# A graph network and a mixture of experts on one core: routing and the picking of the first tile block by block inside the attention projection

## The chip, the cores and the metric

The kernel runs on one core of a Trainium2 chip. The metric is the device time of one execution in microseconds (us), median of three runs.

The engines are named as in the profile. PE (TensorE) multiplies matrices and PEld loads its weights. DVE (VectorE), ACT (ScalarE) and POOL (GpSimd) work on elements. SP (SyncE) only issues transfers here, and so do the queues of ACT and POOL.

## The reference, cut to what matters

```python
x = x + gnn(_layernorm(x), ...)                  # two graph convolutions over 10,000 edges, 625 nodes, D = 768
x = x + ffn(_layernorm(x)[None], ...)[0]

def ffn(x, ...):                                 # H = 12 heads of 64, E = 8 experts, K = 1, DF = 3072
    h = _ln(x, ln1_g, ln1_b)
    ...                                          # q, k, v, causal softmax, out
    x = x + out @ Wp + bp                        # the attention projection
    h2 = _ln(x, ln2_g, ln2_b).reshape(-1, d)
    gate_logits = h2 @ Wg
    w, sel = jax.lax.top_k(gate_logits, K)
    w = jax.nn.softmax(w, axis=-1)
    combine = jnp.zeros((n, E)).at[jnp.arange(n)[:, None], sel].add(w)
    hid = jax.nn.relu(jnp.einsum('nd,edf->enf', h2, W1) + b1[:, None, :])
    y = jnp.einsum('enf,efd->end', hid, W2) + b2[:, None, :]
    return x + jnp.einsum('ne,end->nd', combine, y)
```

## The kernel before

The 625 rows of x stand in five blocks (C = 5) of 125 rows (P = 125), one row to a partition. Every large product is made from high and low parts: a matrix a is cut into hi(a), rounded, and lo(a) = a - hi(a), and a product is three matmuls (hi hi, hi lo, lo hi). ACT makes the high parts (helper `hi`, L599), DVE the low ones (helper `lo`, L892 and L894).

There is no scheduler. Each engine has its own program, in the order in which it is written, and the engines wait for each other on counting semaphores (`s_...`). So an instruction that waits holds up all that stands behind it on its engine.

The stages are: one-hot counts of the edges and the two graph layers, the projections of q, k and v, attention, the attention projection with `Wp`, then the experts. The places that matter here:

- **Attention projection** (PE, `rows_product`, L1323): for each block 36 matmuls (72 with both parts of the rows, in two halves of 384 columns). DVE adds the residual (L1146, tile x2), takes the row statistics (L927 to L929), the root comes from ACT (L606), and the normalized block n2 is written in L931. PE turns n2 (`turn_n2`, L1589), ACT scales it with the second norm's weights (`h2_turned`, L798, tile h2T), and PE multiplies it with Wg (`gate_products`, L1596).
- **Routing**, for all five blocks at once after the last block: DVE copies the gate logits, finds maximum and index (L1158 to L1167) and makes a mark of the chosen expert (L1170). PE counts with it how many rows ahead chose the same expert (L1619, ranks, and L1622, totals). DVE computes from it each row's own place, 128 places (CAP) for each expert (L1194 to L1203), and the marks of the first tile (L1206, tile oh0).
- **First tile**: PE picks the rows of expert 0 by multiplying n2 with these marks (L1639, thirty matmuls), ACT scales them (L819, hgf) and makes the high part, DVE the low part (tiles hgh, hgl). All other tiles come through memory: POOL sends every row of n2 to its place in hs_d (L548, an indirect DMA for each block), and reads tile after tile back (L554).
- **Weights**: SP brings chunks of 128x2304 (`raw`, four buffers), 16 for each expert: eight of W1 and eight of W2. Chunk n + 4 is asked for when the low part of chunk n is made. ACT makes whi (L599), DVE wlo (L894), four buffers of each.
- **Expert tile** (`tile`): eight times W1 (PE, L1675), each result copied (ACT, L850), turned (PE, L1648 to L1662) and biased (DVE, L1258, tile bia), cut into parts (hTT), and eight times W2 (PE, L1694). The result goes to ys_d (POOL, L559).
- **Filler**: `keep_busy` (L1330) issues matmuls whose result nobody reads; TURN_BUSY is 24, CHOICE_BUSY 50.
- **The end**: POOL gathers the result rows of experts 0 to 6 (L563), DVE adds them (L1279). The last expert's result stays in PSUM: it is cut into parts, PE spreads it to the rows with turned marks (`spread_y`, L1715, tile oh7T), after it has put each row's bias b2 there with turned marks of all experts (`bias_y`, L1710, tile oh8T). DVE multiplies by the row's weight and adds the base (L1289), and SP stores the block.

## Time and profile before

| what | value |
|---|---|
| time, median of 3 runs | 928.65 us (924.72 to 932.22) |
| profiled execution, its own time | 930.92 us |
| span in the profile | 929.4 us, mean granted clock 0.971 |
| PE busy | 874.0 us (94%) |
| DVE busy | 705.7 us (76%) |
| ACT busy | 556.4 us (60%) |
| POOL busy | 90.3 us (10%) |

The span is the time from the first to the last instruction in the trace. A busy share is an average over stages with different limits. The granted clock is a share of TensorE's full 2.4 GHz.

### The profile page before, as it was taken

The page shows a single profiled execution, that of the slowest core. Times are in us where ns is not written, and L with a number is a line of the kernel's source. Part 1 is how long each engine was busy: PE and PEld are TensorE (multiplying, and loading weights), DVE is VectorE, ACT ScalarE, POOL GpSimd, SP SyncE. Part 2 cuts the span into 40 slices and gives each one's busy share as a digit, 9 for nine tenths or more (in the row PEclk, how much of TensorE's full clock was granted, in tenths as well). Part 3 has the DMA queues.
Part 4 walks back from the last instruction along what each step waited for, and adds up shares of the span by engine and source line. Part 5 has one row for each costly group of instructions (what it writes and reads, how often), then busy time and mean ns, then how long its engine had stood idle before and what let it go on. Part 6 is the DMA issues. An engine that isn't in the chain of part 4 may idle for free.

```text
span 929.4 us, 14804 instructions
## 1 busy us (share of the span) xinstructions
PE 874.0 (94%) x5460; PEld 842.0 (91%) x5460; DVE 705.7 (76%) x1060; ACT 556.4 (60%) x780; POOL 90.3 (10%) x88
## 2 busy tenths in 40 slices
PE   7999898989998888899889999999999999999998
PEld 7899897989998667689889989999999999999996
DVE  7997155784333899855559889898998989898895
ACT  5503223154323788842548778787887878787870
POOL 2000006031000400012050000000000000000041
PEclk9999788999999999999799999999999999999998
DMA  7020006348114910060189999999999999999984
GB/s 228 3 101 1 1 2 119 85 101 183 55 51 112 326 71 2 1 185 1 36 254 327 331 349 354 376 335 377 363 361 377 354 378 344 379 358 368 369 288 130
...
## 3 DMA queue, kind: packets, MB, share of 16 engines
...
## 4 chain that ended last, share of the span: by engine, by line
PE 43%; DVE 29%; DMA 13%; issue 7%; ACT 7%; SPq 0%; DVEq 0%; ACTq 0%
DVE wlo L894 14%; PE ps L1323 13%; DMA raw<-in_L_ffn_W 12%; PE ps L1499 7%; PE ps L1675 5%; PE ps L1694 5%; ACT whi L599 3%; DVE pr L1094 2%; DVE hTT L892 2%; DVE pTl L894 2%; PE ps L1352 1%; PE ps L1559 1%; DVE pr L1101 1%; DVE ohs L945 1%; DMA xs<-in_x 1%
## 5 line engine op out<-in xcount | busy, mean ns | idle before, releaser
L894 DVE TENSOR_TENSOR wlo<-raw,whi 128x2304 fp32r<-128x2304 f32 x137 | 350.9, 2570 | 23.7 <-ACT whi L599 23.5
L599 ACT ACTIVATE whi<-raw 128x2304 fp32r<-128x2304 f32 x139 | 296.2, 2132 | 83.4 <-DMA raw<-in_L_ffn_W 34.3
L1694 PE MATMUL ps<-whi,hTT 128*128 128x384 f32 x768 | 201.6, 339 | 1.0 <-ACT oh7T L599 1.0
L1694 PEld LDWEIGHTS ps<-whi,hTT 128*128 128x128 f32 x768 | 139.2, 188 | 1.2 <-ACT oh7T L599 1.2
L1675 PE MATMUL ps<-whi,hgh 128*128 128x384 f32 x384 | 134.1, 349 | 2.8 <-DVE hgl L894 2.8
L1675 PE MATMUL ps<-whi,hgl 128*128 128x384 f32 x384 | 130.3, 339 | 0.0
L1675 PE MATMUL ps<-wlo,hgh 128*128 128x384 f32 x384 | 129.8, 338 | 0.0
L1694 PE MATMUL ps<-wlo,hTT 128*128 128x384 f32 x384 | 129.0, 336 | 0.0
L1675 PEld LDWEIGHTS ps<-whi,hgh 128*128 128x128 f32 x384 | 73.3, 191 | 2.9 <-DVE hgl L894 2.9
L1675 PEld LDWEIGHTS ps<-wlo,hgh 128*128 128x128 f32 x384 | 73.2, 191 | 0.0
L1675 PEld LDWEIGHTS ps<-whi,hgl 128*128 128x128 f32 x384 | 73.0, 190 | 0.0
L1694 PEld LDWEIGHTS ps<-wlo,hTT 128*128 128x128 f32 x384 | 72.3, 188 | 0.0
L1352 PE MATMUL ps<-ohd,ohs 125*125 125x314 bf16 x400 | 58.2, 304 | 7.7 <-DVE ohd L946 5.7
L1352 PEld LDWEIGHTS ps<-ohd,ohs 125*125 125x125 bf16 x400 | 53.8, 139 | 10.9 <-DVE ohd L946 9.0
L1258 DVE TENSOR_TENSOR bia<-ps,b1T 128x384 f32<-128x384 f32 x64 | 35.6, 556 | 16.2 <-PE ps L1662 16.2
L606 ACT ACTIVATE root<-var 125x2 f32<-125x2 f32 (+2 forms) x13 | 2.7, 204 | 67.0 <-DVE var L914 66.9
L894 DVE TENSOR_TENSOR ql<-ps,qh 64x125 fp32r<-64x125 f32 (+1 forms) x66 | 21.8, 331 | 26.5 <-ACT qh L599 25.4
L1536 PE MATMUL ps<-ident,pr 125*125 125x125 f32 x168 | 30.6, 300 | 12.1 <-DVE pr L1101 7.6
L1536 PEld LDWEIGHTS ps<-ident,pr 125*125 125x125 f32 x168 | 22.4, 189 | 20.5 <-DVE pr L1101 9.5
L892 DVE SCALAR_TENSOR_TENSOR hTT<-bia,hTT 128x384 fp32r<-128x384 f32 x64 | 35.5, 554 | 5.6 <-ACT hTT L599 5.6
L599 ACT ACTIVATE qh<-ps 64x125 fp32r<-64x125 f32 (+1 forms) x66 | 20.1, 305 | 31.9 <-PE ps L1499 23.0
L756 ACT ACTIVATE pr<-pr,negmax 125x126 f32<-125x126 f32 (+4 forms) x60 | 36.0, 600 | 2.2 <-DVE negmax L1094 1.5
...
## 6 DMA issues: line engine op xcount, KB each, us to landing
raw<-in_L_ffn_W SPq DMA_DIRECT2D x128, 1152.0 KB, 6.9
...
```

Of the source, the lines that this page charges most:

```text
L599: act.activation(out_, in_, func).then_inc(s, 1)
L756: act.activation(pr[:, u % PRS, 0:n], pr[:, u % PRS, 0:n], ACT.Exp, bias=negmax[:, u % 4, :], scale=-1.0, accum_out=ssum[:, u // 2 % 2, u ...
L892: dve.scalar_tensor_tensor(out_, in_, 0.0, hi_, ALU.max, ALU.subtract).then_inc(s, 1)
L894: dve.tensor_tensor(out_, in_, hi_, ALU.subtract).then_inc(s, 1)
L1094: dve.tensor_tensor_reduce(pr[:, u % PRS, 0:n], score_rows(u)[:, 0:n], cmask[:, (C - 1 - c) * P:(C - 1 - c) * P + n], -(float(D) ** -0.5), ...
L1258: dve.tensor_tensor(bia[:, k % 2, :, :], blocks(2 + k % 2, 128, JW, CAP), bcol.rearrange("p (j o) -> p j o", o=1).broadcast_to((128, JW, C ...
L1323: ins = mm(ps[0:P, bank + half, 0:HB], l, rr, start=m == 0 and i == 0, stop=m == DC - 1 and i == 2)
L1352: ins = mm(ps[0:P, m, 0:HALF], ohs[:, i % EU, m * P:(m + 1) * P], ohd[:, i % EU, :], start=i in BOUNDS, stop=i + 1 in BOUNDS)
L1499: ins = mm(ps[:, 2 * (m % 2) + half, 0:HALF], l, rr, start=c == 0 and i == 0, stop=c == DC - 1 and i == 2)
L1536: ins = nc.tensor.transpose(turned_part(u)[:, b, :], pr[:, u % PRS, b * P:(b + 1) * P], ident[0:P, 0:P])
L1675: ins = mm(ps[0:CAP, k % 2, 0:FW], l, rr, start=m == 0 and j == 0, stop=m == DC - 1 and j == 2)
L1694: ins = mm(ps[0:CAP, 4 + half, 0:HB], l, rr, start=k == 0 and j == 0 and jj == 0, stop=k == FCH - 1 and j == JW - 1 and jj == 2)
```

## The change

The routing is done by blocks. `gate_products(c)` of blocks 0 to 2 runs in the middle of the product of block c + 2, DVE chooses (`chosen`) and places (`placed`) single blocks, PE counts ranks by blocks, and the picking matmuls of the first tile (`choice`) run by blocks too, into six banks. Half of the picked tile is scaled by DVE, and its high and low parts are made in two halves. The fillers get new places and numbers. The low parts of the first two weight chunks are made by POOL. The rest of the routing (totals, spill-over, slots for the scatter) stands on DVE behind the low part of the first tile.

The turned marks oh8T and the bias matmuls go. Instead POOL gathers for each block the bias row of its chosen expert from b2 (`bias_rows`) into x2, and DVE adds it, times the row's weight, to the base during the first tile. The row weights (an exponential on ACT, a division on DVE) are made in the first tile as well.

```diff
+POOL_LOW = 2
+HALF_IN = DC // 2
+CHOICE_BANK = (6, 7, 4, 5, 0, 1)
...
-TURN_BUSY = 24
-CHOICE_BUSY = 50
+NORM_BUSY = 40
+GATE_BUSY = 8
+SPLIT_BUSY = 30
...
+            def bias_rows(c):
+                g.wait_ge(s_oh8, 2 * c + 1)
+                g.wait_ge(s_n2, c + 1)
+                g.wait_ge(s_base, c + 1)
+                g.indirect_dma_start(out=x2[:, c, :], out_offset=None, in_=b2[:, :],
+                                     in_offset=bass.IndirectOffsetOnAxis(ap=eidx[:, c:c + 1], axis=0)
+                                     ).then_inc(s_b2g[c], 16)
+            for c in range(C):
+                g.wait_ge(s_x2, c + 1)
+                gp.tensor_tensor(base[:, c, :], base[:, c, :], x2[:, c, :], ALU.add).then_inc(s_base, 1)
+                if c >= 2:
+                    bias_rows(c - 2)
+            for n in range(POOL_LOW):
+                g.wait_ge(s_mhi, n + 1)
+                gp.tensor_tensor(wlo[n][:, :], raw[n][:, :], whi[n][:, :], ALU.subtract).then_inc(s_mlo, 1)
             g.wait_ge(s_zero, 16 * (TILES + 2 + K_OVER))
             g.wait_ge(s_slot, 1)
             g.wait_ge(s_n2, C)
             for c in range(C):
                 g.indirect_dma_start(out=hs_d[:, :], out_offset=bass.IndirectOffsetOnAxis(ap=slot[:, c:c + 1], axis=0),
                                      in_=n2[:, c, :], in_offset=None).then_inc(s_scat, 16)
+            for c in range(C - 2, C):
+                bias_rows(c)
...
             for c in range(C):
-                root_of()
                 if c >= 1:
                     h2_turned(c - 1)
-            h2_turned(C - 1)
+                root_of()
             a.wait_ge(s_x2, C)
             split_hi(0, 0)
-            a.wait_ge(s_oh8, 1)
-            act.activation(rt[:, 7, 0:C], rt[:, 6, 0:C], ACT.Exp).then_inc(s_act, 1)
+            h2_turned(C - 1)
             split_hi(1, 0)
             split_hi(2, 0)
...
-            tile_part(1, range(DC))
-            tile_hi(DC)
-            split_hi(3, 0)
+            a.wait_ge(s_hgT, 1)
+            for m in range(HALF_IN):
+                act.activation(hgf[:, m, :], first_in(m), ACT.Identity, scale=lnT[:, 2 * DC + m:2 * DC + m + 1],
+                               bias=lnT[:, 3 * DC + m:3 * DC + m + 1]).then_inc(s_hga, 1)
+            a.wait_ge(s_hga, HALF_IN)
+            hi(hg[0][:, 0:HALF_IN, :], hgf[:, 0:HALF_IN, :], s_hgh)
+            a.wait_ge(s_hgb, DC - HALF_IN)
+            hi(hg[0][:, HALF_IN:, :], hgf[:, HALF_IN:, :], s_hgh)
...
                             a.wait_ge(s_scat, 16 * C)
                         hi(hTT_part(0, k - 2), bia[:, k % 2, :, :], s_hTh2, ACT.Relu)
-                    if first and k - 2 == OVER_N2:
+                    if first and k == FCH:
+                        a.wait_ge(s_oh8, 2 * C)
+                        act.activation(rt[:, 7, 0:C], rt[:, 6, 0:C], ACT.Exp).then_inc(s_act, 1)
+                    if first and k == FCH + 6:
                         a.wait_ge(s_ohT, 1)
-                        hi(oh8T[0:E, :, :], blocks(4, E, C, P), s_ohl)
-                        hi(oh7T[:, :, :], blocks(6, 128, C, P), s_ohl)
+                        hi(oh7T[:, :, :], blocks(0, 128, C, P), s_ohl)
...
-            a.wait_ge(s_b2in, 16)
-            a.wait_ge(s_used, SCH * (E - 1) + FCH + 6)
-            hi(b2h, bc[1][0:E, :], s_b2h)
...
+            def chosen(c):
+                d.wait_ge(s_gate, c + 1)
+                dve.tensor_copy(lg[:, c, :], ps[0:P, 2, c * E:(c + 1) * E]).then_inc(s_lg, 1)
+                d.wait_ge(s_lg, c + 1)
+                step(dve.max(mx8[:, c, :], lg[:, c, :]))
+                step(dve.max_index(ix8[:, c, :], mx8[:, c, :], lg[:, c, :]))
+                step(dve.tensor_copy(ef5[:, c:c + 1], ix8[:, c, 0:1]))
+                dve.tensor_copy(eidx[:, c:c + 1], ix8[:, c, 0:1])
+                for to in (ohb, ohe):
+                    dve.tensor_scalar(to[:, c, :], iota8[:, :], ef5[:, c:c + 1], None, ALU.is_equal).then_inc(s_oh8, 1)
+            def placed(c0, c1):
+                d.wait_ge(s_rank, c1)
+                d.wait_ge(s_oh8, 2 * c1)
+                dve.tensor_tensor(prod[:, c0:c1, :], rank8[:, c0:c1, :], ohe[:, c0:c1, :], ALU.mult
+                                  ).then_inc(s_rkread, c1 - c0)
+                d.wait_ge(s_rkread, c1)
+                step(dve.reduce_sum(rank[:, c0:c1], prod[:, c0:c1, :], AX))
+                step(dve.scalar_tensor_tensor(own[:, c0:c1], ef5[:, c0:c1], float(CAP), rank[:, c0:c1],
+                                              ALU.mult, ALU.add))
+                for c in range(c0, c1):
+                    dve.tensor_scalar(oh0[:, c, :], iotac[:, :], own[:, c:c + 1], None, ALU.is_equal).then_inc(s_oh0, 1)
+            normed_rows(0)
+            normed_rows(1)
+            chosen(0)
+            normed_rows(2)
+            chosen(1)
+            normed_rows(3)
+            chosen(2)
+            normed_rows(4)
+            d.wait_ge(s_iotac, 1)
+            placed(0, 3)
+            chosen(3)
+            placed(3, 4)
+            chosen(4)
+            placed(4, 5)
+            d.wait_ge(s_hgT, 1)
+            for m in range(HALF_IN, DC):
+                dve.tensor_scalar(hgf[:, m, :], first_in(m), lnT[:, 2 * DC + m:2 * DC + m + 1],
+                                  lnT[:, 3 * DC + m:3 * DC + m + 1], ALU.mult, ALU.add).then_inc(s_hgb, 1)
+            for i, part in enumerate((slice(0, HALF_IN), slice(HALF_IN, DC))):
+                d.wait_ge(s_hgh, i + 1)
+                lo(hg[1][:, part, :], hgf[:, part, :], hg[0][:, part, :], s_hgl)
+            d.wait_ge(s_rank, C + 1)
...
-            split_lo(1, 0)
-            split_lo(2, 0)
-            tile_in(1)
-            for c in range(C):
-                dve.tensor_scalar(oh0[:, c, :], iotac[:, :], float(CAP * (E - 1)), own[:, c:c + 1],
-                                  ALU.add, ALU.is_equal).then_inc(s_ohe, 1)
-            split_lo(3, 0)
+            d.wait_ge(s_mlo, POOL_LOW)
...
+                    if first and k == FCH + 2:
+                        for c in range(C):
+                            dve.tensor_scalar(oh0[:, c, :], iotac[:, :], float(CAP * (E - 1)), own[:, c:c + 1],
+                                              ALU.add, ALU.is_equal).then_inc(s_ohe, 1)
+                        d.wait_ge(s_act, 1)
+                        step(dve.reciprocal(rt[:, 7, 8:8 + C], rt[:, 7, 0:C]))
+                        step(dve.tensor_tensor(wtok[:, :], rt[:, 7, 0:C], rt[:, 7, 8:8 + C], ALU.mult))
+                    if first and FCH + 3 <= k < FCH + 3 + C:
+                        c = k - FCH - 3
+                        d.wait_ge(s_base, c + 1)
+                        d.wait_ge(s_b2g[c], 16)
+                        dve.scalar_tensor_tensor(base[:, c, :], x2[:, c, :], wtok[:, c:c + 1], base[:, c, :],
+                                                 ALU.mult, ALU.add).then_inc(s_base2, 1)
...
+                d.wait_ge(s_base2, c + 1)
                 d.wait_ge(s_yg[c], 16)
                 dve.scalar_tensor_tensor(base[:, c, :], x2[:, c, :], wtok[:, c:c + 1], base[:, c, :],
                                          ALU.mult, ALU.add).then_inc(s_yin, 1)
+            for c in range(C - 1):
+                others_y(c)
             for half in range(2):
                 d.wait_ge(s_yh, half + 1)
                 part = slice(half * HB, (half + 1) * HB)
                 lo(wlo[0][0:CAP, part], ps[0:CAP, 4 + half, 0:HB], whi[0][0:CAP, part], s_yl)
-            d.wait_ge(s_yin, C)
-            for c in range(C):
+            others_y(C - 1)
+            for c in range(C):
+                d.wait_ge(s_yin, c + 1)
...
+            def ranks(c):
+                pe.wait_ge(s_oh8, 2 * c + 1)
+                if c >= 3:
+                    pe.wait_ge(s_rkread, c)
+                for b in range(c + 1):
+                    ins = mm(ps[0:P, 3, c * E:(c + 1) * E], before[:, :] if b == c else onesb[:, :], ohb[:, b, :],
+                             start=b == 0, stop=b == c)
+                ins.then_inc(s_rank, 1)
+            def choice(c, part):
+                pe.wait_ge(s_oh0, c + 1)
+                for m in part:
+                    ins = mm(first_in(m), n2[:, c, m * 128:(m + 1) * 128], oh0[:, c, :], start=c == 0, stop=c == C - 1)
                 return ins
+            def busy(n, bank):
+                keep_busy(n, onesb[:, :], onesb[:, :], bank)
             pe.wait_ge(s_wg, 16)
             for c in range(C):
                 if c >= 2:
                     pe.wait_ge(s_x2, c - 1)
-                rows_product(q, 2 * WP, c, 4 + 2 * (c % 2), None if c else {DC - 1: (s_pvl, 2 * STEPS)}).then_inc(s_wp, 1)
-                if c >= 2:
-                    gate_products(c - 2)
+                rows_product(q, 2 * WP, c, 4 + 2 * (c % 2), None if c else {DC - 1: (s_pvl, 2 * STEPS)},
+                             (lambda b=c - 2: gate_products(b)) if c >= 2 else None).then_inc(s_wp, 1)
                 if c >= 1:
                     turn_n2(c - 1)
-            keep_busy(TURN_BUSY, onesb[:, :], onesb[:, :], 3)
-            turn_n2(C - 1)
-            gate_products(C - 2)
-            gate_products(C - 1).then_inc(s_gate, 1)
-            keep_busy(TURN_BUSY, onesb[:, :], onesb[:, :], 3)
-            pe.wait_ge(s_oh8, 1)
-            ohb = rt[:, 4, 0:C * E // 2].bitcast(BF16).rearrange("p (c e) -> p c e", e=E)
-            for c in range(C):
-                for b in range(c + 1):
-                    mm(ps[0:P, 3, c * E:(c + 1) * E], before[:, :] if b == c else onesb[:, :], ohb[:, b, :],
-                       start=b == 0, stop=b == c)
+                if c >= 2:
+                    ranks(c - 2)
+            pe.wait_ge(s_x2, 4)
+            busy(NORM_BUSY, 7)
+            gate_products(3)
+            turn_n2(4)
+            busy(GATE_BUSY, 7)
+            pe.wait_ge(s_x2, C)
+            choice(0, range(4))
+            ranks(3)
+            choice(1, range(4))
+            gate_products(4)
+            choice(2, range(4))
+            for c in range(3):
+                choice(c, range(4, DC))
+            ranks(4)
+            pe.wait_ge(s_lg, C)
             for b in range(C):
-                ins = mm(ps[0:P, 3, C * E:(C + 1) * E], onesb[:, :], ohb[:, b, :], start=b == 0, stop=b == C - 1)
+                ins = mm(ps[0:P, 2, C * E:(C + 1) * E], onesb[:, :], ohb[:, b, :], start=b == 0, stop=b == C - 1)
             ins.then_inc(s_rank, 1)
+            choice(3, range(DC))
+            choice(4, range(DC)).then_inc(s_hgT, 1)
+            pe.wait_ge(s_rkread, C)
+            busy(SPLIT_BUSY, 3)
...
-            def bias_y(c, half):
-                for i, t in enumerate((b2h, b2l)):
-                    mm(ps[0:P, LAST_BANK[c] + half, 0:HB], oh8T[0:E, c, :], t[:, half * HB:(half + 1) * HB],
-                       start=i == 0, stop=False)
             def spread_y(c, half):
                 for i, t in enumerate((whi[0], wlo[0])):
                     ins = mm(ps[0:P, LAST_BANK[c] + half, 0:HB], oh7T[:, c, :], t[0:CAP, half * HB:(half + 1) * HB],
-                             start=False, stop=i == 1)
+                             start=i == 0, stop=i == 1)
                 return ins
-            pe.wait_ge(s_b2l, 1)
-            pe.wait_ge(s_hga, DC * (E + 1))
-            for c in range(3):
-                for half in range(2):
-                    bias_y(c, half)
+            pe.wait_ge(s_ohl, 1)
+            pe.wait_ge(s_hga, DC * E + HALF_IN)
```

POOL, from the residual sums to the sending of the rows; before:

```order
L538 TENSOR_TENSOR base<-base,x 125x768 [waits x2_made] x4
L542 IOTA iotac 125x128 [waits heads_done]
L548 DMA hs_d<-n,slot 1664x768 [waits n2_made,rows_chosen,hs_zeroed]
L548 DMA hs_d<-n,slot 1664x768 x4
L554 DMA hs<-hs_d 128x768 [waits tile_turned,tokens_sent]
```

and now:

```order
L558 TENSOR_TENSOR base<-base,x 125x768 [waits x2_made]
L552 DMA x<-in_L_ffn_b,eidx 125x768 [waits base_made,n2_made,choice_made]
L563 TENSOR_TENSOR wlo<-raw,whi 128x2304 [waits expert_hi] x2
L568 DMA hs_d<-n,slot 1664x768 [waits n2_made,rows_chosen,hs_zeroed]
L568 DMA hs_d<-n,slot 1664x768 x4
L552 DMA x<-in_L_ffn_b,eidx 125x768 [waits base_made,n2_made,choice_made] x2
L576 DMA hs<-hs_d 128x768 [waits tile_turned,tokens_sent]
```

Two low parts and five gathers of bias rows have come in, two of these gathers behind the scatter.

DVE, from the choice of the experts to the marks of the first tile; before, five blocks at once, with a low part of the weights in between:

```order
L1170 TENSOR_TENSOR rt<-iota,rt 125x40
L1175 RECIPROCAL rt<-rt 125x5 [waits scalar_steps,choice_made]
L1176 TENSOR_TENSOR wtok<-rt 125x5 [waits vector_steps]
L894 TENSOR_TENSOR wlo<-raw,whi 128x2304 [waits expert_hi]
L1194 TENSOR_TENSOR rt<-ps,capk 125x32 [waits ranks_done]
L1196 TENSOR_TENSOR rt<-ps,rt 125x40
L1197 TENSOR_REDUCE rt<-rt 125x8 [waits vector_steps]
L1198 TENSOR_REDUCE rt<-rt 125x5
L1201 TENSOR_TENSOR tp<-tri,rt 125x64 [waits vector_steps]
L1203 SCALAR_TENSOR_TENSOR rt<-rt 125x5
L1206 TENSOR_SCALAR oh<-iotac,rt 125x128 [waits slots_numbered,vector_steps]
```

and now, the placing of blocks 0 to 2 and the choosing of block 3:

```order
L1202 TENSOR_TENSOR rt<-ps,rt 125x24 [waits ranks_done,choice_made,slots_numbered]
L1205 TENSOR_REDUCE rt<-rt 125x3 [waits ranks_read]
L1206 SCALAR_TENSOR_TENSOR rt<-rt 125x3 [waits vector_steps]
L1209 TENSOR_SCALAR oh<-iotac,rt 125x128 [waits vector_steps]
L1209 TENSOR_SCALAR oh<-iotac,rt 125x128 x2
L1189 COPY rt<-ps 125x8 [waits gates_done]
L1191 MAX rt<-rt 125x8 [waits gates_read]
L1192 MAX_INDEX rt<-rt 125x8 [waits vector_steps]
L1193 CAST rt<-rt 125x1 [waits vector_steps]
L1194 CAST eidx<-rt 125x1 [waits vector_steps]
L1196 TENSOR_SCALAR rt<-iota,rt 125x8 x2
```

The step L1206 (now) computes the own places from two tiles in SBUF; the marks L1209 follow it. The low part of the weights is gone from between them.

DVE in the second half of the first tile (the chunks of W2), now:

```order
L1310 TENSOR_SCALAR oh<-iotac,rt 125x128 x5
L1313 RECIPROCAL rt<-rt 125x5 [waits scalar_steps]
L1314 TENSOR_TENSOR wtok<-rt 125x5 [waits vector_steps]
L917 TENSOR_TENSOR wlo<-raw,whi 128x2304 [waits expert_hi,vector_steps]
L1319 SCALAR_TENSOR_TENSOR base<-x,wtok,base 125x768 [waits b2_in0,base_made]
```

Before, only low parts stood there; the marks of the last expert and the row weights were made ahead of or early in the tile, and the base additions with bias rows did not exist.

## Rows read from the trace of the kernel before

**Rows 1.** Busy time by stretch: head, tile 0 in two parts, a middle tile
```profile
core 0: us, PE busy (x) PEld busy (x) DVE busy (x) ACT busy (x) POOL busy (x), PEclk, DMA share, GB/s
444.60:475.20 30.60, 25.15 (x249) 24.81 (x248) 18.68 (x66) 16.07 (x26) 11.19 (x6) 0.83 0.35 106
475.20:506.60 31.40, 30.39 (x176) 29.64 (x176) 25.13 (x26) 22.22 (x24) 4.93 (x3) 0.95 0.93 306
506.60:534.10 27.50, 27.50 (x162) 27.43 (x163) 22.58 (x13) 20.66 (x18) 0.58 (x1) 1.00 0.96 329
...
649.30:703.20 53.90, 53.55 (x319) 52.89 (x318) 49.10 (x35) 43.75 (x41) 1.08 (x2) 1.00 1.03 364
```

**Rows 2.** Chain of waits, 444 to 488: start us, us, what
```profile
444.58 0.97 DVE x L1146
...
447.27 2.08 ACT h2T L798 x6
...
452.60 2.53 PE ps L1596 x12
...
459.82 4.49 PE ps L1330 x50
464.31 6.77 PE ps L1639 x60
471.10 2.21 ACT hgf L819 x6
...
475.22 8.09 PE ps L1675 x36
...
484.70 3.13 PE ps L1675 x18
```

**Rows 3.** Timeline of ACT and DVE, 447 to 466: start us, us, instruction
```profile
447.06 0.20 ACT L606 ACTIVATE root<-var 125x1 f32<-125x1 f32 x1 [5.95 <-DVE var L914]
...
448.08 0.68 DVE L931 TENSOR_SCALAR n<-x,mv,rstd 125x768 f32<-125x768 f32 x1
...
452.41 2.15 ACT L599 ACTIVATE whi<-raw 128x2304 fp32r<-128x2304 f32 x1
...
460.47 0.19 DVE L1196 TENSOR_TENSOR rt<-ps,rt 125x40 f32<-125x40 f32 x1
...
461.35 1.07 DVE L1206 TENSOR_SCALAR oh<-iotac,rt 125x128 f32<-125x128 f32 x5
...
465.09 5.01 DVE L894 TENSOR_TENSOR wlo<-raw,whi 128x2304 fp32r<-128x2304 f32 x2
```

**Rows 4.** POOL and DVE side by side (timelines; xN rows: ns min/median/max, first and last start)
```profile
L538 POOL TENSOR_TENSOR base<-base,x x5: 1812/1830/1843, 416.1 to 445.6; 125x768 f32<-125x768 f32 x5
...
179.81 2.14 POOL L510 TENSOR_TENSOR xf<-xf,bc 125x768 f32<-125x768 f32 x1 [22.85 <-DVE n L1058]
...
180.88 1.02 DVE L1036 SCALAR_TENSOR_TENSOR xs<-ps,dinv,xs 125x768 f32<-125x768 f32 x1 [0.63 <-PE ps L1323]
...
193.02 2.21 POOL L510 TENSOR_TENSOR xf<-xf,bc 125x768 f32<-125x768 f32 x1 [4.75 <-DVE n L1058]
...
193.44 2.58 DVE L894 TENSOR_TENSOR hTl<-aff,hTh 128x750 fp32r<-128x750 f32 x1
...
L894 DVE TENSOR_TENSOR hTl<-aff,hTh x5: 934/943/2584, 193.4 to 215.6; 128x750 fp32r<-128x750 f32 x5
...
L894 DVE TENSOR_TENSOR wlo<-raw,whi x2: 3367/3782/4197, 143.4 to 146.7; 128x2304 fp32r<-128x2304 f32 x2
```

**Rows 5.** Timeline of DVE in tile 0: bias steps of two chunks in a row, end
```profile
491.67 0.56 DVE L1258 TENSOR_TENSOR bia<-ps,b1T 128x384 f32<-128x384 f32 x1
...
495.13 0.56 DVE L1258 TENSOR_TENSOR bia<-ps,b1T 128x384 f32<-128x384 f32 x1
...
533.87 0.55 DVE L1246 COPY ysb<-ps 128x384 f32<-128x384 f32 x1
```

**Rows 6.** Chain of waits, the end
```profile
913.95 2.30 PE ps L1710 x12
...
924.82 1.02 DVE base L1289
```

134 lines of the change are left out of this document (53 added, 81 removed).

## The prediction

> **What bounds the kernel now.** I read first the table of stretches [rows 1], for who is busy in which stage, then the chain of waits through the routing [rows 2] and at the end [rows 6], then the timeline of the engines for the steps that are moved [rows 3, 5], and last the places where POOL and DVE compute at the same time [rows 4].
>
> In a middle expert (649.3 to 703.2) TensorE is busy 53.55 of 53.9 us and DVE only 49.10; DMA shows a share above 1 at 364 GB/s. A started expert stage is bound by TensorE, with little room in the DMA, and a shift of its start goes through to the end if the weights keep up. From 444.6 to 475.2 no expert work is done: DMA share 0.35, granted clock 0.83. That TensorE is "busy" there is mostly filler, 4.49 us of it in one row [rows 2]. The chain goes from the last block's sum (444.58) through normalization, gate products (2.53 us at the lower clock), ranks, the picking of the first tile (6.77 us), its scaling on ACT (2.21 us) and its high and low parts to the first expert matmul at 475.22. That is 30.6 us. What this change can gain is there, in tile 0 behind it, and in the end after 913.95.
>
> **The head, step by step.** (a) Routing of blocks 0 to 2 is now done inside the projection. The fifth product has one more gate product in front of it (half of 2.53 us, so 1.25) and three rank matmuls (fillers of like form take 4.49/50 = 0.09 us each), with waits some 1.9 us. So it ends near 446.5 and not 444.58. (b) On ACT the last root now stands behind the scaling of block 3 (2.1 us, [rows 2]), which costs some 0.6 us more: root at 449.6 for 447.06, and the last normalized block, which was done 1.70 us after the root's start (448.08 + 0.68, [rows 3]), is done at 451.3 for 448.76. (c) Ranks by marks and own slots took 460.47 to 462.42 for five blocks [rows 3]; for the first three 1.4 us, so their first-tile marks could be ready at 452.7. (d) What is left per block is small: choosing (copy, maximum, index, marks) 1.2 us and placing 0.9 us on DVE, and on TensorE 0.23 us for each of the thirty picking matmuls (6.77/30). Most of them run while DVE chooses; behind the last mark only the last block's six stand, and ahead of those block 3's six. With nothing else in the way I come to a tile picked at 462.7. (e) Behind it half of the scaling goes to DVE (three of six on each), and the high and low parts are cut in two: 1.1 + 0.4 + 0.5 + latencies of 0.4 = 2.4 us in place of 475.22 - 471.08 = 4.1. First expert matmul: 465.1, 10 us earlier.
>
> **What POOL does to it.** The two first low parts (128x2304) go from DVE (2.5 us each, 5.01/2 [rows 3]) to POOL. POOL's add of 125x768 takes 1.83 us [rows 4], so three times as many elements take 5.5 us. It can begin when ACT has made the high part. ACT does it straight behind the last root, 449.8 to 452.0. So POOL works from about 452.1 to 457.6, and on the second one (high part done near 457.2, behind the last block's scaling) until 463.3. This is just when DVE runs the short steps for blocks 3 and 4. The rows say what two such engines do to each other: DVE's hTl takes 0.94 us as a rule, but 2.58 when it starts at 193.44 inside POOL's add of 193.02 to 195.23, that is, it begins its work when POOL ends. At 143.4 and 146.7, beside other adds of POOL, two wlo took 3.37 and 4.20 us for 2.5; the second is longer by 1.7, one POOL add. The DVE step at 180.88, with one input from PSUM, ran inside POOL's add unhindered in 1.02 us. So a DVE step with two inputs from SBUF waits for the end of POOL's instruction, however short it is itself. The step that makes the own slots is of this kind, once for block 3 and once for block 4; the tensor_scalar marks may be (POOL's add at 179.81 took 2.14 for 1.83, with such a step ahead of it). The Trainium skill (SBUF — State Buffer, "Who interferes with whom") says the same: the shared pair of ports is held for a whole instruction, by DVE with two SBUF inputs or in a two-port mode, and the other engine blocks. By that page the marks (fp32 tensor_scalar, SBUF to SBUF) block as well, and its sum would be the forecast's or the second rival's, never the first's; the trace agrees for the two-input form.
>
> So in the likeliest course the marks of blocks 0 to 2 just get through, block 3's own slots wait until the first POOL instruction ends at 457.8, what follows in that block until 463.4, and block 4 comes behind: placing 0.4, choosing 1.2, ten rank matmuls 0.6, twelve picking matmuls 2.7, scaling and split 2.4, and 1 to 2 us because TensorE has waited 4 to 6 us there and, as behind 475.22 after 2.8 us of idleness (granted 0.95 over that stretch, [rows 1]), comes back at the lower clock. First expert matmul at about 472.4: **2.8 us earlier**, not 10. If nothing blocked it would be -10.1; if DVE gets one mark through each time it is later than before (rivals).
>
> **Tile 0.** Before, it ran from 475.22 to 533.87 [rows 5], 58.6 us, against 53.9 of a later one. The first 36 matmuls took 8.09 us where 18 take 3.13 at the full clock [rows 2]: 1.8 us for the clock. Now thirty fillers reach to within 1 us of the start; I count 1.5 of the 1.8 as gained. Five of ten mark transposes go, and so does the wait for their copy at the turn from W1 to W2, together 1.7 us. Against it: DVE gets five base additions (1.02 us, by 180.88 and 924.82), the marks, and weights of the tokens, 6.5 us more from chunk 12 on. It was busy 22.6 of 27.5 us there [rows 1], so most fits into what was idle, but its lead is thinner than before. Its routing rest (4 us) and the low parts 2 and 3 (5 us) now lie behind the first tile's start, and in W1 it goes at 3.46 us a chunk (491.67 to 495.13), TensorE's own pace, so it can't catch up. I take 3.5 us lost at the turn to tile 1 (bounds 0 and 6.5), and 0.5 us in tiles 1 and 2, since the token rows and two blocks of bias rows now travel while the DMA is at 0.93 to 0.96. Tile 0 and behind: -1.5 - 1.7 + 3.5 + 0.5 = **+0.8** (from -3 to +4). Splitting the bias rows, which goes too, was done while TensorE still worked on the last expert, and I count it at nothing.
>
> **The end.** Twelve bias matmuls (2.30 us) stood between the last expert matmul and the spreading [rows 6], and four times two more between the later spreadings; now the bias rows are in the base already. The last low half is ready 1.3 us after 913.9, the fifth base addition is behind it (1.02), and then five output steps of 1.02 us follow each other: 913.9 + 1.3 + 1.0 + 5.0 = 921.2 for 925.84 (924.82 + 1.02). Of these 4.6 us the output DMAs, now closer together, take back some 0.4. **-4.2** (bounds -2.3, the first row alone, and -5).
>
> **Sum.** -2.8 + 0.8 - 4.2 = -6.2. The profiled execution took 930.92 us (span 929.4 and 1.5 around it), 2.3 above the median of 928.65; the same step down from the median gives 922.4, which I round to **922 us**, with a range of its own of 917 to 927.
>
> **Rivals.** (1) Nothing blocks: the short steps are not of the kind that waits, or DVE is always first. For it: only the two-input form is shown to wait, and the DVE step at 180.88 did not. Against it: own slots are that very form. Head -10.1, sum -13.5: 915. (2) Slower: POOL takes the ports between two marks. The first mark of block 0 starts by my count 0.1 us ahead of POOL's first low part. If POOL comes in behind it, the second mark waits 5.5 us, the third another 5.5, the choosing of block 3 begins at 463.3, and gate product, picking and ranks follow in TensorE's order, partly at half clock: first expert matmul at 483, +8. Sum +8 + 0.8 - 4.2 = +4.6: 933. At 146.7 one POOL add did come in between two wlo that stood back to back [rows 4]. It decides if the first picking is not over before POOL starts. (3) The feed becomes the bound: the third and fourth low parts come 7 to 9 us behind the first expert matmul, where before the third was made ahead of it (465.09 to 470.10), so tile 0 waits for its weights and the earlier start is given back. Head -2.8, feed +4.5 more than counted: 927. (4) The fillers: 78 in place of 98, in places where TensorE waits anyway; more than 1 us either way is not in them, so it gets no chance of its own.
>
> **Chances.** Forecast 0.50, no blocking 0.23, feed 0.15, marks cut by POOL 0.12. Eight times in ten the time should be from 914 to 931: the lower end leaves out the better half of the first rival, the upper one most of the second. A measurement of this kernel tells about 1% from no change (9.3 us; the three runs lie 7.5 apart). Faster by over 1% (under 919.4): the first rival and a fifth of the forecast, with a little for what I undercount at the end, 0.36. Slower by over 1%: the worst third of the second rival and something unforeseen, 0.06. Within 1%: 0.58.
>
> **What would show it.** In the profile after: the first expert matmul at 472 (465: rival 1; 480 or more: rival 2); POOL's two low parts of 5.5 us; DVE's own-slot steps (125x1) that last some us in place of 0.16; TensorE idle between the picking of block 0 and the ranks of block 3 or 4; the end of tile 0 and its DVE waits; 7.3 us from the last expert matmul to the last output step's end, for 11.9. I am wrong if POOL's low part is much shorter than 5.5 us, if ACT's order delays it past the marks of block 4, or if the feed costs more than 5 us.

## The result and the profile after

The changed kernel takes 943.2 us (median of 4 runs, 938.79 to 947.46), the kernel before 927.1 in the runs beside it: ratio 1.0166, 95% interval 1.0099 to 1.0232. It is 16 us slower; the prediction said 6 us faster. Its profiled execution took 947.46 us, with a span of 945.9.

First the table of stretches of the changed kernel, cut at the same events as [rows 1]: last block's sum to first expert matmul, the two halves of tile 0, and a middle expert.

```profile
core 0: us, PE busy (x) PEld busy (x) DVE busy (x) ACT busy (x) POOL busy (x), PEclk, DMA share, GB/s
448.30:482.10 33.80, 24.42 (x192) 23.79 (x190) 19.94 (x45) 12.85 (x22) 13.09 (x4) 0.65 0.25 82
482.10:517.60 35.50, 30.43 (x162) 29.33 (x162) 28.75 (x41) 18.98 (x18) 18.17 (x8) 0.90 0.84 265
517.60:553.10 35.50, 31.45 (x172) 31.35 (x173) 29.11 (x27) 26.54 (x25) 0.58 (x1) 0.90 0.87 303
668.50:722.40 53.90, 53.90 (x320) 53.60 (x319) 49.42 (x35) 43.74 (x41) 1.08 (x2) 1.00 1.03 365
```

The head takes 33.8 us for 30.6, at a granted clock of 0.65 for 0.83. Tile 0 takes 71.0 us for 58.6, and in it TensorE waits some 9 us. A middle expert is as before. So the loss has two places, and the larger one is tile 0.

The chain of waits through the head (compare [rows 2]):

```profile
450.99 0.23 ACT root L628
...
453.44 10.21 DVE oh L1209 x3
...
464.77 0.59 PE ps L1668 x4
465.36 1.91 PE ps L1676 x8
467.27 2.32 PE ps L1656 x12
469.60 4.47 PE ps L1676 x20
...
475.04 4.66 PE ps L1676 x24
...
479.72 1.16 ACT hgf L848 x3
480.91 0.53 ACT hgh L621
481.46 1.03 DVE hgl L917 x2
```

Three marks of 128 columns, 0.21 us each in [rows 3], take 10.21 us. TensorE waits meanwhile, and behind them nearly all runs at the lower level of its clock (granted 0.54 from 464.8 to 480): the last twelve picking matmuls (24 records, two for each) take 4.66 us, where they take 2.80 in the kernel e3 below, and a gate product takes 2.32. The timeline at this place, POOL and DVE side by side, and behind it the two lines by themselves (shortest, median and longest in ns):

```profile
453.31 10.06 POOL L563 TENSOR_TENSOR wlo<-raw,whi 128x2304 fp32r<-128x2304 f32 x2 [0.76 <-ACT whi L621]
453.44 10.21 DVE L1209 TENSOR_SCALAR oh<-iotac,rt 125x128 f32<-125x128 f32 x3
```

```profile
L1209 DVE TENSOR_SCALAR oh<-iotac,rt x5: 273/289/5094, 453.4 to 475.1; 125x128 f32<-125x128 f32 x5
...
L563 POOL TENSOR_TENSOR wlo<-raw,whi x2: 5042/5045/5048, 453.3 to 458.3; 128x2304 fp32r<-128x2304 f32 x2
```

POOL's first low part began 0.13 us ahead of the first mark. That mark took 5.00 us and ended 0.09 us behind POOL's first instruction; the second took 5.09 us, through POOL's second one; the third took 0.27. So each of the two waited for one POOL instruction.

In tile 0 the chain stands on two transfers of weights, and POOL's queue shows what else travelled then:

```profile
488.47 9.01 DMA raw<-in_L_ffn_W
...
504.10 14.91 DMA raw<-in_L_ffn_W
```

```profile
498.62 1.18 POOL L568 DMA_INDIRECT hs_d<-n,slot  x1 [0.30 <-issue]
500.11 1.21 POOL L552 DMA_INDIRECT x<-in_L_ffn_b,eidx  x1 [0.30 <-issue]
501.63 3.54 POOL L552 DMA_INDIRECT x<-in_L_ffn_b,eidx  x1 [0.30 <-issue]
```

A chunk of weights lands 6.8 us after its issue as a rule. The one that was asked for at 504.10, right behind the last two gathers of bias rows (L552), came 14.9 us later. DVE has its stall there, too: 4.43 us ahead of the hTT step at 522.04.

The end (compare [rows 6]), in the chain and in the timeline:

```profile
923.16 8.18 DMA x<-ys_d,slot
...
933.05 2.35 PE ps L1792 x12
```

```profile
934.80 4.71 DVE L1345 SCALAR_TENSOR_TENSOR base<-ps,wtok,base 125x768 f32<-125x768 f32 x5
...
935.84 5.93 SPq L464 DMA_DIRECT2D out_x<-base  x10
```

From the last expert matmul (932.8) to the end of the fifth output step (939.5) it is 6.7 us for 11.9. But the span ends at 945.9, 6.4 us behind that step, where it was 3.6: the ten output transfers are now issued within 5.9 us (8.0 before) and still have to be carried, with the DMA engines at a share of 0.80 to 0.94 until 943. The end gains 2.4 us, not 4.2.

The account of the 16.5 us between the two profiled executions: 2.0 lie ahead of anything the change touches (the first block's sum is at 417.00 for 414.99), 1.7 in the longer projection, 3.2 in the head, 12.4 in tile 0, -2.4 in the end, and some -0.4 in the other tiles.

### The profile page after: what moved, and what is told of

It reads as the page before. It is cut to its first block, busy times and chain, and to the rows that moved or that the text cites. A ratio compares the mean times of both kernels' runs of the same rounds, so it can differ in the third digit from the quotient of the medians.

```text
span 945.9 us, 14729 instructions
## 1 busy us (share of the span) xinstructions
PE 874.0 (92%) x5391; PEld 844.8 (89%) x5391; DVE 722.0 (76%) x1092; ACT 554.3 (59%) x776; POOL 107.3 (11%) x94
## 4 chain that ended last, share of the span: by engine, by line
PE 62%; DVE 20%; DMA 7%; issue 5%; ACT 5%; POOL 1%; DVEq 0%; SPq 0%; ACTq 0%; POOLq 0%
PE ps L1759 14%; PE ps L1774 14%; PE ps L1381 12%; PE ps L1557 7%; DMA raw<-in_L_ffn_W 6%; DVE wlo L917 5%; PE ps L1410 4%; PE ps L1744 2%; DVE pr L1117 2%; PE ps L1617 2%; DVE pTl L917 2%; PE ps L1594 1%; PE ps L1676 1%; DVE pr L1124 1%; DVE oh L1209 1%
## 5 line engine op out<-in xcount | busy, mean ns | idle before, releaser
L917 DVE TENSOR_TENSOR wlo<-raw,whi 128x2304 fp32r<-128x2304 f32 x135 | 345.4, 2568 | 19.9 <-ACT whi L621 19.8
L1774 PE MATMUL ps<-whi,hTT 128*128 128x384 f32 x768 | 205.4, 343 | 0.0
L1774 PEld LDWEIGHTS ps<-whi,hTT 128*128 128x128 f32 x768 | 141.6, 189 | 0.0
L1744 PE MATMUL ps<-ident,hid 128*128 128x128 f32 x192 | 32.6, 279 | 13.0 <-ACT hid L874 12.9
L917 DVE TENSOR_TENSOR ql<-ps,qh 64x125 fp32r<-64x125 f32 (+1 forms) x66 | 21.8, 331 | 26.7 <-ACT qh L621 25.7
L1594 PEld LDWEIGHTS ps<-ident,pr 125*125 125x125 f32 x168 | 23.8, 202 | 19.6 <-DVE pr L1124 9.5
L1744 PEld LDWEIGHTS ps<-ident,hid 128*128 128x128 f32 x192 | 24.6, 143 | 17.5 <-ACT hid L874 15.7
```

Source lines behind the costliest of these rows:

```text
L917: dve.tensor_tensor(out_, in_, hi_, ALU.subtract).then_inc(s, 1)
L1594: ins = nc.tensor.transpose(turned_part(u)[:, b, :], pr[:, u % PRS, b * P:(b + 1) * P], ident[0:P, 0:P])
L1744: ins = nc.tensor.transpose(blocks(2 + k % 2, 128, JW, CAP)[:, j, :], hid[0:CAP, k % 2, j * 128:(j + 1) * 128], ident[0:CAP, 0:CAP])
L1774: ins = mm(ps[0:CAP, 4 + half, 0:HB], l, rr, start=k == 0 and j == 0 and jj == 0, stop=k == FCH - 1 and j == JW - 1 and jj == 2)
```

## The experiments

Each run was timed beside the kernel before, whose median was 927.1 us for e1 to e4, 925.2 for e5 to e8, 925.7 for e9 to e12 and 925.8 for e13 to e15; the ratios are to these, with their 95% intervals. Two measures are taken from all traces: **head**, from the last block's sum to the first expert matmul, and **tile 0**, from there to DVE's first copy of its result. Before: 30.6 and 58.6. After: 33.8 and 71.0. Other stretches differ from execution to execution: the first block's sum, ahead of all that was changed, lies at 410.9 to 417.0 in the 17 traces (414.99 before). So I compare these two stretches, and not whole spans.

### Who blocks the marks (e1, e2, e3)

**e1_pool_after_marks.** POOL waits for all marks before its low parts.

```diff
+            g.wait_ge(s_oh0, C)
             for n in range(POOL_LOW):
```

> The changed kernel, but POOL starts its two low parts only when all five blocks have their first-tile marks (a wait for the fifth mark). Theory 1 (ports: the marks waited for POOL's instructions): the three marks of blocks 0 to 2 take 0.7 us instead of 10.2, the fifth mark is made some 12 us earlier, and the first expert matmul comes 8 to 11 us earlier, held only by POOL's first low part behind the marks. Theory 2 (feed: tile 0 is long, 71.0 us for 58.6, because the third and fourth low parts and with them the requests for chunks 6 and 7 come late): tile 0 stays at 68 us or more, since those low parts move with the rest. Sum: 930 to 936 us for 943. If the marks waited for something else, the head does not move and the time stays near 943.

**e2_pool_pieces.** Each low part in six instructions of 384 columns.

```diff
-                gp.tensor_tensor(wlo[n][:, :], raw[n][:, :], whi[n][:, :], ALU.subtract).then_inc(s_mlo, 1)
+                for j in range(6):
+                    cols = slice(j * CH // 6, (j + 1) * CH // 6)
+                    ins = gp.tensor_tensor(wlo[n][:, cols], raw[n][:, cols], whi[n][:, cols], ALU.subtract)
+                ins.then_inc(s_mlo, 1)
```

> The changed kernel, but POOL makes each of the two low parts in six instructions of 128x384 instead of one of 128x2304; same engine, same data, same order. Theory 1 (a DVE step waits for the end of the POOL instruction that is running): a mark waits at most 0.84 us, the three marks take 1 to 3 us instead of 10.2, first expert matmul 8 to 11 us earlier. If POOL's work as a whole and not the single instruction blocks DVE, or if the marks waited for data, they still take 10 us. Theory 2 (feed): chunk 4 and 5 are asked for as before, 6 and 7 some 9 us earlier together with the first expert matmul, tile 0 is 66 to 71 us. Sum: 930 to 936 us.

**e3_dve_low.** DVE makes both, in places where it waits for TensorE.

```diff
-            for n in range(POOL_LOW):
-                g.wait_ge(s_mhi, n + 1)
-                gp.tensor_tensor(wlo[n][:, :], raw[n][:, :], whi[n][:, :], ALU.subtract).then_inc(s_mlo, 1)
...
             placed(3, 4)
+            split_lo(0, 0)
             chosen(4)
             placed(4, 5)
+            split_lo(1, 0)
```

> The changed kernel, but DVE makes all low parts: that of chunk 0 between the placing of block 3 and the choosing of block 4, that of chunk 1 behind the placing of block 4. POOL has none. Theory 1: marks in 0.7 us, first expert matmul near 468 on the changed kernel's time axis, 13 to 15 us earlier than 482. Theory 2: the requests for chunks 4 and 5 stay near 460 and 465, the third and fourth low parts still stand behind the routing's rest, so tile 0 stays longer than 62 us; 64 to 70. Sum: 922 to 929 us. A rival to theory 2 (the bias rows and the token rows load the DMA in tile 0) says the same of this run, and is told apart by the next one.

Measured: e1 935.11 us, ratio 1.0095 (1.0064 to 1.0127); e2 936.48, 1.0114 (1.0064 to 1.0164); e3 929.15, 1.0021 (0.9997 to 1.0044). The marks and POOL in the timelines, e1:

```profile
450.09 0.68 DVE L1210 TENSOR_SCALAR oh<-iotac,rt 125x128 f32<-125x128 f32 x3
...
458.07 10.42 POOL L564 TENSOR_TENSOR wlo<-raw,whi 128x2304 fp32r<-128x2304 f32 x2 [8.88 <-DVE oh L1210]
...
461.92 7.00 DVE L918 TENSOR_TENSOR hgl<-hgf,hgh 128x384 fp32r<-128x384 f32 x2 [0.69 <-ACT hgh L622]
```

e2:

```profile
452.79 9.60 POOL L565 TENSOR_TENSOR wlo<-raw,whi 128x384 fp32r<-128x384 f32 x10 [0.77 <-ACT whi L624]
...
452.90 2.88 DVE L1212 TENSOR_SCALAR oh<-iotac,rt 125x128 f32<-125x128 f32 x3
```

and e3:

```profile
451.62 0.68 DVE L1206 TENSOR_SCALAR oh<-iotac,rt 125x128 f32<-125x128 f32 x3
...
464.25 0.44 PE L1757 MATMUL ps<-whi,hgh 128*128 128x384 f32 x1 [0.65 <-DVE hgl L914]
```

The same three marks: 10.21 us beside whole low parts, 2.88 beside pieces of a sixth, 0.68 beside none. The wait goes with the length of POOL's instruction. e1 only moves it: now the tile's own low parts (two steps, 1.03 us in e3) take 7.00. In e2 the own-slot step of block 3, whose inputs are both in SBUF, takes 0.45 us where 0.16 is usual, so that form waits as well; in the changed kernel it began each time while POOL was idle. The head: e1 18.7 (15 us shorter, where 8 to 11 were expected), e2 23.8, e3 17.8 us. The unblocked head of the prediction was 18.6 (446.5 to 465.1); that part of the working was right. With e3's head 16 us shorter than after's, 13 shorter than before's, the kernel is still no faster than before. Tile 0 takes 75.1 us in e1, 70.9 in e2 and 70.5 in e3: what was gained ahead of the first matmul is lost behind it.

### Bias rows alone (e4, e8, e11, e13)

**e4_before_bias_rows.** The kernel before, with the rows of b2 gathered by POOL behind the request for the second tile's rows, added by DVE in tile 0, and without the turned marks and the bias matmuls at the end.

```diff
             next_in(0)
+            for c in range(C):
+                g.wait_ge(s_base, c + 1)
+                g.indirect_dma_start(out=x2[:, c, :], out_offset=None, in_=b2[:, :],
+                                     in_offset=bass.IndirectOffsetOnAxis(ap=eidx[:, c:c + 1], axis=0)
+                                     ).then_inc(s_b2g[c], 16)
...
+                    if first and FCH + 3 <= k < FCH + 3 + C:
...
+                        dve.scalar_tensor_tensor(base[:, c, :], x2[:, c, :], wtok[:, c:c + 1], base[:, c, :],
```

> The kernel before with one part of the change alone: bias rows gathered by POOL for each block (all five behind the request for the second tile), added to the base by DVE in tile 0, and no bias matmuls, no marks of all experts, at the end. Theory 2 (feed by late low parts): tile 0 grows by 0 to 3 us for 1.9 MB of rows and 5 us of DVE work; the end is 2 to 4 us shorter; sum 924 to 928 for 927. Rival (the gathers of bias rows make tile 0 long): tile 0 grows by 5 to 12 us and the time is 930 to 937.

Measured 938.53 us, 1.0127 (1.0090 to 1.0165), head 31.5, tile 0 68.5. Nothing of the head's change is in it, and it is 11 us slower, more than the rival expected. In the chain of e4 a chunk's transfer is one step of 18.38 us, and in the table of stretches:

```profile
492.00:514.00 22.00, 14.45 (x76) 13.74 (x75) 12.60 (x10) 8.91 (x10) 9.46 (x3) 0.92 1.04 266
```

The DMA engines are full, 1.04, and carry 266 GB/s. A middle expert has the same share at 365.

**e8_additions_only.** e4 without the five gathers; the additions stay, on what lies there.

> The kernel of e4_before_bias_rows (938.53, 11 us over before, tile 0 68.5 us for 58.6) without the five gathers; DVE's five additions to the base stay, on what lies in x2 (so the bias of the second product is wrong in the output). Theory G (the gathers): tile 0 back to 58 to 61 us, and the shorter end stays, total 924 to 928. Theory D (DVE's additions in W2 of tile 0 cost it the lead): 934 to 938.

Measured 923.97 us, 0.9991 (0.9964 to 1.0019), head 30.6, tile 0 57.7; the longest transfer in the chain of tile 0 is 8.39 us. So DVE's additions cost nothing measurable there, and the gathers cost 10.7 us of tile 0. The stretch of the same place:

```profile
488.00:510.00 22.00, 21.42 (x128) 20.41 (x128) 20.68 (x18) 17.38 (x19) 0.57 (x1) 1.00 0.95 329
```

**e11_rows_from_many** and **e13_rows_direct** ask what in the gathers is dear: many reads of eight rows, the indirect form, or the volume. e11 keeps the indirect form and reads `hs_d` by `slot` in place of `b2` by `eidx`; the edit of e13 on e4:

```diff
-                g.indirect_dma_start(out=x2[:, c, :], out_offset=None, in_=b2[:, :],
-                                     in_offset=bass.IndirectOffsetOnAxis(ap=eidx[:, c:c + 1], axis=0)
-                                     ).then_inc(s_b2g[c], 16)
+                g.dma_start(x2[:, c, :], hs_d[c * P:(c + 1) * P, :]).then_inc(s_b2g[c], 16)
```

> The kernel of e4 (938.53, 1.0127) with its five gathers taken from as many different rows of another table of the same width (the scattered token rows, read back by slot), in the same place, volume and number of descriptors; the output's bias is wrong. Theory R (the slowness comes from 625 reads of the same eight rows of b2): DMA at 350 or more at a full share in the stretch of the gathers, tile 0 62 to 64 us, ratio 1.003 to 1.007. Theory V (volume and the form of an indirect gather, whatever the rows): as e4, 1.011 to 1.015.

> The kernel of e4 (1.0127 of before) and e11 (1.0085) with the five transfers as plain DMAs of the same 384 KB each, from consecutive rows of the token rows' table, in the same place on POOL's queue (the output's bias is wrong). In both others the DMA engines were full behind 492 us and moved only 255 to 265 GB/s, and tile 0 took 68.5 us. Theory V (volume: 1.92 MB more in a stretch in which the DMA is full): as before, 68 us for tile 0, 1.008 to 1.013. Theory I (the indirect form of the gather, not its volume): 350 GB/s or more, tile 0 near 62 to 64 us, 1.000 to 1.005.

Measured: e11 935.7 us, 1.0085 (1.0046 to 1.0124), tile 0 68.6; e13 934.56, 1.0116 (1.0079 to 1.0154), tile 0 68.2. Their stretches, e11:

```profile
492.00:514.00 22.00, 13.66 (x71) 12.67 (x70) 11.34 (x10) 9.15 (x12) 6.71 (x3) 0.88 1.03 263
```

and e13, where the five transfers are issued within 2.7 us from 486.62:

```profile
490.00:502.00 12.00, 8.35 (x47) 8.00 (x46) 7.89 (x7) 4.95 (x6) 0.00 (x0) 0.94 1.03 274
```

All three forms behave alike in tile 0. e11's timed ratio alone fell between the two theories, and its interval overlaps that of e4; the trace decides for the volume, in the sense that neither the eight rows nor the indirect form is the cause. The volume alone does not explain the size, though: 1.92 MB at the weights' 365 GB/s are 5.3 us, and tile 0 grew by 10 to 11. In the 22 us of e4 the engines carried 266 GB/s where they carry 365 when as full, 2.2 MB less. Why such rows beside weights lower the rate of full engines stays open. All three forms load 125 rows of 3 KB into SBUF from POOL's queue, behind each other; another queue, another number of rows or pauses between them were not tried.

### Bias rows in the new order (e5, e6, e12)

**e5_no_bias_rows** is e3, **e12_after_no_bias_rows** is the changed kernel itself, both without gathers and additions; **e6_rows_early** is e3 with the last two gathers ahead of the scatters, in the head, where the DMA share is 0.34 in e3. e5 and e12 leave the bias of the second product out.

```diff
+            for c in range(C - 2, C):
+                bias_rows(c)
             g.wait_ge(s_zero, 16 * (TILES + 2 + K_OVER))
             g.wait_ge(s_slot, 1)
...
-            for c in range(C - 2, C):
-                bias_rows(c)
```

> The kernel of the run e3_dve_low without the bias rows: no gather of b2's rows and no addition of them to the base (the bias of the second product is left out of the output). In e3 the first expert matmul was ready at 465 us, 10 us ahead of before, and the total was the same, 929.15; tile 0 took 70 us. Theory G (the gathers slow the weights: in the stretches with bias-row gathers the DMA engines were full and moved only 250 to 290 GB/s, where 370 to 400 are moved at the same share without them): two of five gathers leave tile 0, DMA back at 350 or more, tile 0 down by 4 to 6 us, total 923 to 925. Theory F (feed order: chunks 6 and 7 are requested late because their raw buffers come free only behind the routing's rest on DVE): less than 2 us gained, 927 to 929.

> The changed kernel itself without gathers and additions of bias rows (left out of the output), with POOL's two low parts as they are. It took 1.0166 of before. Theory G: 5 to 7 us less, ratio 1.009 to 1.011: the rest of the loss is the head (the marks behind POOL, first expert matmul near 480) and the late requests of chunks 6 and 7. If in this kernel chunk 6 is requested so late that the gathers are over by then, almost nothing: 1.014 to 1.017.

> The kernel of e3 with the gathers of the last two blocks' bias rows ahead of the scatters on POOL's queue, at about 455 and 460 us, where the DMA is nearly idle. Theory G: both leave the stretch in which weights stream, as in e5, so most of e5's gain without leaving anything out: 924 to 927. Theory F: 928 to 930, no change. A rival within G: the gathers are slow wherever they are and delay the scatters behind them, then tile 1's rows come late: 930 to 933.

Measured: e5 918.91 us, 0.9922 (0.9896 to 0.9949), tile 0 61.5; e12 934.68, 1.0076 (1.0043 to 1.0109), head 33.7, tile 0 61.8; e6 922.74, 0.9970 (0.9948 to 0.9992), tile 0 63.3. Against the before beside it, e5 is below the range of theory G (923 to 925 beside 927.1 is 0.9956 to 0.9978) and so is e12; e6 is within it (0.9967 to 0.9999). Stretches behind 490, e3's and e6's:

```profile
496.00:500.00 4.00, 2.49 (x16) 2.17 (x15) 2.29 (x3) 2.92 (x3) 0.62 (x1) 1.00 1.05 280
```

```profile
490.00:500.00 10.00, 10.00 (x62) 9.63 (x61) 9.56 (x10) 7.49 (x9) 0.62 (x1) 1.00 1.00 377
```

Over all of 490 to 500, e3 has 305 GB/s at a share of 1.03.

In the changed kernel the bias rows cost 9.2 us of tile 0 (71.0 against 61.8) and 0.9% of the time. Three of five gathers run during the projection and its end; the two behind the scatters make nearly all of the loss. Placed some 30 us earlier (454 and 459 for 486 and 487) they give back 7.2 of e3's 9.0 us, and what is left, under 2 us (63.3 against 61.5), has the other three gathers and the additions in it. Timed, e6 is 0.5% behind e5, 4.4 us, of which the traces show 1.8 in tile 0 and 1.6 in the tiles behind it. For two gathers, 0.77 MB, 7.2 us are over three times the 2.1 us that their bytes take at 364 GB/s.

Rows of this length from this queue do not lower the rate as such. In e5 the scatters send the token rows of all five blocks, as much as five gathers, in the indirect form and by the same queue, from SBUF to memory; 1.83 MB of them travel beside the weights in these 16 us:

```profile
480.00:496.00 16.00, 11.61 (x69) 10.94 (x70) 10.94 (x11) 9.13 (x10) 5.82 (x3) 1.00 1.02 383
```

The full engines carry 383 GB/s there. What differs in the gathers is that they load into SBUF; whether that is the reason is not shown.

### Late low parts, and what is left of the head (e7, e9, e10, e14, e15)

**e7_lo_first.** e3 with the third and fourth low part ahead of the routing's rest.

```diff
+            split_lo(2, 0)
+            split_lo(3, 0)
             d.wait_ge(s_rank, C + 1)
...
-                    if k + 2 < SCH:
+                    if k + 2 < SCH and not (first and k < 2):
                         split_lo(k + 2, t)
```

> The kernel of e3 with the third and fourth low part on DVE ahead of the rest of the routing, so that the raw buffers of chunks 6 and 7 come free 3.5 us earlier (requests at 467 and 470 in place of 470.6 and 473). Theory F: tile 0 shorter by those 3.5 us, total 925 to 926. Theory G: the DMA is full behind 474 anyway, but it starts earlier by 3.5 us on an idle DMA, minus what the later scatters (5 us later) cost: 926 to 929. If the scatters' delay is what decides: 930 to 933.

Measured 923.35 us, 0.9988 (0.9961 to 1.0015), which is theory F's upper end (926 beside 927.1); tile 0 67.0 for e3's 70.5: 3.5 us, as much as the requests come earlier.

**e9_lo_first_rows_early** has the edits of e6 and e7. **e10_bias_at_end** is e7 with the bias as in before: no gathers, mark transposes and bias matmuls back. **e14_head_alone** is e10 without the edit of e7. **e15_additions_in_w1** is e9 with the exponential, the token weights and the additions in the first half of tile 0; its edit, cut to the additions, stands behind the expectation of e14.

> Both edits of e6 and e7 on the kernel of e3: the bias rows of the last two blocks gathered ahead of the scatters, and the third and fourth low part ahead of the routing's rest. Each alone took some 4 us from e3 (0.9970 and 0.9988 of before, for 1.0021). If they cure different losses (G the gathers in the weights' stream, F the late requests of chunks 6 and 7), they add: ratio 0.992 to 0.994, 918 to 920 us where before is 925 to 926. If both are the same loss seen twice: 0.996 to 0.998.

> The kernel of e7 with the bias rows as in before: no gathers, no additions in tile 0, but the mark transposes, the split of b2 and the bias matmuls at the end come back (all of the output is computed). Theory G: tile 0 as in e5 or shorter (61 us, less 2 for the earlier requests), the end longer than e5's by the 2.2 us that the end gained in after: ratio 0.991 to 0.993, as good as e9. If the end gains more than the gathers cost when these are early, it is slower than e9 by 2 us or more.

> The kernel of e10 (0.9931) without the third and fourth low part ahead of the routing's rest: the routing and picking by blocks alone, all low parts on DVE, bias rows at the end as in before. If the earlier requests of chunks 6 and 7 are worth the 3.5 us by which they are earlier: 0.996 to 0.998, a third of the head's 10 us. If the DMA's rate alone sets the end of tile 0: 0.993 to 0.995, as e10.

```diff
-                    if first and FCH + 3 <= k < FCH + 3 + C:
-                        c = k - FCH - 3
+                    if first and 4 <= k < 4 + C:
+                        c = k - 4
```

> The kernel of e9 (0.9903) with exponent, token weights and the five base additions in the first half of tile 0 (chunks 3 to 8), where DVE waits for weights, in place of the second half, where it has none to spare (DMA share 0.84 at 520 to 530, because raw buffers come free late). If DVE is what holds the requests there: DMA share 0.95 or more at 520 to 530, 1 to 3 us less, 0.987 to 0.989. If the additions in the first half delay the low parts as much: 0.990 to 0.993.

Measured: e9 919.91 us, 0.9903 (0.9868 to 0.9938); e10 919.89, 0.9931 (0.9905 to 0.9957); e14 921.08, 0.9962 (0.9940 to 0.9983); e15 918.19, 0.9930 (0.9905 to 0.9955). Tile 0: 61.5, 60.5, 61.6 and 61.2 us; the head 17.6 to 17.8 in all.

All four beat both kernels, the one before by 0.4 to 1.0%. The two cures add: the differences of e6 and e7 from e3 would put e9 at 0.9937, at the edge of its interval. The earlier requests are worth 1.1 us of tile 0 without gathers (61.6 in e14 against 60.5 in e10), not 3.5; timed, the two are 0.3% apart and their intervals overlap. e9 and e10 can't be told apart: early gathers with the shorter end are as good as no gathers with the longer one. e15 shows no gain, neither in the time nor in tile 0 (61.2 for 61.5), so DVE's additions are not the bound in the second half of tile 0. The share that was expected to rise did rise at 520 to 530, from 0.84 to 1.05, but tile 0 ends at 524.0 in e9 and at 521.9 in e15, so most of that stretch is already tile 1.

Head and tile 0 together, 89.3 us before, are 78.1 in e10: 11 us less. Timed, it is 0.7%, 6.4 us. 1.7 of the difference go into the projection. Part of the rest is the end. With the bias matmuls, from the first of them to the end of the last output step, it takes 12.0 us before, 14.2 in e10, and 10.8 in e14, whose code is the same there as e10's. TensorE's granted clock goes with it, here for ten microseconds from the same place in before, e10 and e14:

```profile
915.10:925.10 10.00, 9.68 (x35) 6.55 (x33) 5.22 (x8) 0.00 (x0) 0.00 (x0) 0.77 0.42 133
```

```profile
907.00:917.00 10.00, 10.00 (x32) 6.68 (x30) 4.74 (x5) 0.00 (x0) 0.00 (x0) 0.60 0.38 120
```

```profile
902.20:912.20 10.00, 8.42 (x35) 5.44 (x33) 5.75 (x6) 0.00 (x0) 0.00 (x0) 0.84 0.48 151
```

In e14 head and tile 0 are 10.1 us shorter than before's and 1.7 go into the projection, but it is timed at 3.5 us less. Where the other 5 go stays open; one trace of each kernel does not settle it.

## Why the prediction was wrong

The prediction had -2.8 for the head with the projection, +0.8 for tile 0 and behind, -4.2 for the end. Measured between the two traces are +4.9, +12.0 and -2.4, besides the 2.0 ahead of the change.

**Marks and POOL: the step that failed first.** It read "in the likeliest course the marks of blocks 0 to 2 just get through". The first mark had to start 0.1 us ahead of POOL by my count; it started 0.13 behind. And 0.1 us would not have been enough: the three marks take 0.68 us one behind the other (e3), so by the same count the second and third start behind POOL, and "just get through" holds only if marks do not wait for POOL at all, which the prediction itself left open. The second rival had marks cut by POOL and got 0.12. Its +8 for the first expert matmul was +4.9 (482.08 for 475.22, of which 2.0 are not the change's), and its course was a little other than it said: POOL came in ahead of the first mark, not behind it, and the price was two POOL instructions all the same. What the forecast took for the blocked step, block 3's own slots, waited for nothing (0.16 us at 465.79, behind POOL's end).

The Trainium skill (SBUF — State Buffer, "Who interferes with whom") names tensor_scalar among the kinds that can enter a two-port mode, under conditions for the operands, and so contend with GpSimd. The marks agree: 5.00 and 5.09 us where 0.28 is usual. The POOL low part was 5.04 us, not 5.5.

**Tile 0: the term that was mis-sized most.** "0.5 us in tiles 1 and 2, since the token rows and two blocks of bias rows now travel while the DMA is at 0.93 to 0.96". The bias rows cost 9.2 us (e12 against after; e4 against e8: 10.7 for five gathers). I had read the DMA share of [rows 1] and did not turn it into a price: 1.92 MB at 364 GB/s is already 5.3 us where no room is left, 2.1 for the two late gathers. The rest, the falling rate at a full share, no row of before showed. So even the slow rival's sum, 933, was missed by another 10 us, and the third rival (feed) had the right place and the wrong cause: the third and fourth low part are worth 1 to 3.5 us.

**The rest of tile 0.** Without bias rows it takes 61.8 us for 58.6, so 3.2 more, for 0.3 in the sum (-1.5, -1.7, +3.5): 3 us too low, within the bounds that were given for it. The clock's 1.5 did come back (TensorE's granted clock is 1.00 from 482 to 490). How the rest is shared out between the turns and the late low parts no run separates.

**The end.** -4.2 against -2.4. Twelve spreadings and five additions went as counted (6.7 us to the last output step, 7.3 expected). The term "the output DMAs take back some 0.4" was 2.8: the ten transfers are issued closer together, and the last of them lands 6.4 us behind the last step for 3.6.

**Right:** the projection (+1.9, measured 1.7), scaling and split (2.4, measured 2.4), and the head with nothing in its way (18.6, measured 17.8 in e3).

**Why a head 13 us shorter gives so little** is in no term of the forecast's sum, only in the third rival's words that the earlier start is given back: e3 and before take the same time. The requests for weights do not come 13 us earlier with the head. From the last block's sum to the last of the four requests behind the first chunks it was 34.6 us before and is 26.7 in e14, 7.9 less. In e14 TensorE is busy through the first 10 us of tile 0, and 10.9 of the next 15, in which the DMA share is 1.03 to 1.06. So the first chunks lie ready, and behind them the stream of weights sets the pace; that this makes the whole 3 us is argued, not shown by a run. In e14, without gathers, tile 0 takes 61.6 us for 58.6: 3 of the 13 us are given back, and with gathers in the stream (e3) 12 are.
